# RWKV-style attention and FFN on one core: one reciprocal-root chain per step, and head outputs transposed by DMA

## The reference

```python
xx = jnp.pad(x, ((0, 0), (1, 0), (0, 0)))[:, :T] - x          # token shift
r, k, v = (x + xx*maa_r) @ Wr.T, (x + xx*maa_k) @ Wk.T, (x + xx*maa_v) @ Wv.T
g = silu((x + xx*maa_g) @ Wg.T)
att = rc @ kc * w_mat                                          # per chunk of 64 tokens
yc = att @ vc + rc @ state * wb
new_state = ws * state + kc * wk @ vc
yn = ((y - mu) / sqrt(var + EPS)) * gamma + beta               # per head of 16
x = x + (yn * g) @ Wo.T
x = x + gelu(layernorm(x).astype(f16) @ W0.T + b0).astype(f16) @ W1.T + b1
```

## Time and profile before

| | |
|---|---|
| time, median of 3 runs | 2166.96 µs (2165.43 to 2167.08) |
| the profiled execution's own time | 2165.32 µs |
| its span | 2163.5 µs |
| PE busy | 2073.6 µs (96%) |
| DVE busy | 1874.7 µs (87%) |
| ACT busy | 1169.2 µs (54%) |
| POOL busy | 378.8 µs (18%) |
| DMA queue of SP | 67.9% of the 16 engines' time |
| chain that ended last | PE 52%, DVE 31%, issue 5%, SP's queue 2%, ACT 2% |

### The profile page before, as it was taken

How to read it: one execution, slowest core, us unless ns; L and a number is a source line. 1 busy time by engine, 2 the same in 40 slices (tenths; PEclk the granted TensorE clock), 3 DMA queues, 4 the chain that set the end, 5 groups by cost and what they waited for, 6 DMA issues and landing times.

```text
span 2163.5 us, 58680 instructions
## 1 busy us (share of the span) xinstructions
PE 2073.6 (96%) x24056; PEld 1485.2 (69%) x24056; DVE 1874.7 (87%) x4336; ACT 1169.2 (54%) x1940; POOL 378.8 (18%) x331
## 2 busy tenths in 40 slices
PE   5678999999999999999999999999999999999998
PEld 4456677777667777667777766777776677777665
DVE  6888998888899888889988888998888998888861
ACT  6555455565545565545556554555555455565442
POOL 1111112111111211211121111112111112111120
PEclk8889999999999999999999999999999999999999
DMA  6545667776666777666677766667776667777667
GB/s 206 185 145 158 207 200 224 223 228 201 201 204 206 226 229 220 192 201 208 216 228 223 227 183 210 198 218 229 223 224 186 210 201 222 226 225 206 200 214 238
DMA packets 342987, 452.72 MB, mean 209 GB/s; under 512 B 183872, under 2 KB 221248, under 8 KB 342720
## 3 DMA queue, kind: packets, MB, share of 16 engines
q1 hardware_dynamic: 341088, 448.76, 67.9%
q10 hardware_dynamic: 1632, 0.21, 0.1%
HBM read 316.24 MB, written 25.17 MB: 158 GB/s over the span
## 4 chain that ended last, share of the span: by engine, by line
PE 52%; DVE 31%; issue 5%; SPq 2%; ACT 2%; DMA 1%; DVEq 0%; ACTq 0%
PE F L917 13%; PE F L888 12%; PE sc L719 6%; PE YT L747 6%; DVE mixf L227 6%; DVE att L1114 5%; PE B L719 4%; DVE S L1137 4%; PE YT L719 3%; DVE att L1108 3%; DVE mix L287 3%; DVE kv L1123 2%; PE B L868 2%; DVE gT L1144 1%; DVE dx L218 1%
## 5 line engine op out<-in xcount | busy, mean ns | idle before, releaser
L888 PE MATMUL F<-xT,ring 128*128 128x256 f16 x4096 | 484.9, 273 | 9.2 <-ACT hT L1396 3.6
L917 PE MATMUL F<-ring,hT 128*128 128x512 f16 x2016 | 475.3, 379 | 1.4 <-ACT hT L1396 1.4
L888 PEld LDWEIGHTS F<-xT,ring 128*128 128x128 f16 x4096 | 396.2, 98 | 72.5 <-issue 7.4
L917 PEld LDWEIGHTS F<-ring,hT 128*128 128x128 f16 x2016 | 189.6, 98 | 200.6 <-ACT hT L1396 3.3
L283 ACT ACTIVATE mix<-mixf 128x1024 f16<-128x1024 f32 x128 | 135.2, 1056 | 326.9 <-DVE mixf L227 213.8
L1396 ACT ACTIVATE hT<-F,b,f_rho 128x256 f16<-128x256 f32 x512 | 260.5, 565 | 36.4 <-PE F L888 36.2
L227 DVE SCALAR_TENSOR_TENSOR mixf<-dx,maa,xnT 128x256 f32<-128x256 f32 x512 | 270.7, 556 | 0.4 <-PEq L492 0.3
L719 PE MATMUL B<-mix,WT 128*128 128x256 f16 x2304 | 269.6, 274 | 0.0
L1519 POOL TENSOR_TENSOR Shl<-S,Shl 128x512 f16<-128x512 f32 x128 | 153.8, 1202 | 657.2 <-ACT Shl L1363 657.2
L719 PEld LDWEIGHTS B<-mix,WT 128*128 128x128 f16 x2304 | 223.9, 98 | 36.1 <-issue 0.2
L1363 ACT ACTIVATE Shl<-S 128x512 f16<-128x512 f32 x128 | 80.2, 627 | 239.0 <-DVE S L1137 131.9
(11 more groups left out here) (175 smaller groups left out, 3037.5 us busy)
## 6 DMA issues: line engine op xcount, KB each, us to landing
ring<-w_dram SPq DMA_DIRECT2D x512, 512.0 KB, 4.6
kx<-kT SPq DMA_DIRECT2D x96, 256.0 KB, 2.5
rx<-rT SPq DMA_DIRECT2D x96, 256.0 KB, 4.4
xa<-in_L_attn_x SPq DMA_DIRECT2D x32, 512.0 KB, 7.4
vbd<-vN SPq DMA_DIRECT2D x256, 64.0 KB, 2.8
x<-in_L_attn_x SPq DMA_DIRECT2D x32, 512.0 KB, 5.4
out<-x SPq DMA_DIRECT2D x31, 512.0 KB, 3.9
ring<-in_L_ffn_W SPq DMA_DIRECT2D x10, 512.0 KB, 8.5
```

What stands on the lines that cost most here:

```text
L888: mm = eng.matmul(F[:, j % 2, i * BT:(i + 1) * BT], ring[:, use % RING, i, a * C + kk * P:a * C + (kk + 1) * P], xT[:, :, kk, :], start=(k ...
L917: mm = eng.matmul(F[:, t, :], hT[:, k, rows(t)], ring[:, use % RING, i, a * C:(a + 1) * C], start=(k == 0 and a == 0), stop=(k == NH - 1 a ...
```

## The change

Two things are changed together.

First, the three chains become one. `rs_a`, `rs_r` and `rs_t` hold, side by side, 2 columns for the rows of block n+1, 64 for the heads of block n-1, and 2 for the FFN rows of block n-2. One chain of 11 instructions over 68 columns runs in step n (`dve_power_half`), and one `dve_row_mean` gives both layer norms their offset. So the FFN's mean and root for block n-2, which before were ready at the end of step n-1, come in step n.

Second, in steps 3 to 31 the 8 PE transposes of y go. ACT splits y into half words in `ygT` (`act_y_words`), SP issues a DMA transpose back into `y` (`sp_y_words`), ACT joins the halves in `ygT` (`act_y_join`), and `act_gated` reads `ygT` instead of `sc`. The gate `gT` gets three halves in place of two, since a gate now lives longer. For these steps the orders of ACT, SP and DVE are written anew (`act_steady`, `sp_steady`, `dve_chunks`); PE's order only loses the transposes. In 28 of the 29 steps (3 to 30) there is a block n+1, and so an x to split, transpose and join.

```diff
+    def dve_power_half(eng, n, k):
+        first, last = has(n)
+        if k == 0:
+            eng.wait_ge(s_va, n + 2)
+            if first <= HEADS <= last:
+                eng.wait_ge(s_gn, n)
+        at = slice(EDGES[first], EDGES[last + 1])
+        rsqrt_step(eng, k, s_rs, RSQRT_STEPS * (n + 1), rs_a[:, at], rs_r[:, at], rs_t[:, at])
...
+    def act_y_words(eng, n):
+        eng.wait_ge(s_yn, NT * (n + 1))
+        eng.wait_ge(s_ygl, NT * n)
+        for h in range(2):
+            eng.activation(y_words[:, h * NT * C:(h + 1) * NT * C].rearrange("p (t c) -> p t c", t=NT),
+                           halves(y[:, :, :])[:, :, :, h], ACT.Copy).then_inc(s_yw, 1)
+    def act_y_join(eng, n):
+        eng.wait_ge(s_ywT, 16 * (n + 2 - BY_DMA))
...
+    def act_steady(eng, n, ahead):
+        act_K_hi(eng, n, 0)
+        act_mix_hi(eng, n, 2)
+        act_K_hi(eng, n, 1)
+        act_fnorm(eng, n - 2)
+        act_R_hi(eng, n, 0)
+        if ahead:
+            act_norm(eng, n + 1)
+            act_x_words(eng, n + 1)
+        act_R_hi(eng, n, 1)
+        act_mix_hi(eng, n, 3)
+        act_y_words(eng, n - 1)
+        act_V_hi(eng, n, 0)
+        act_vw_hi(eng, n, 0)
+        act_gelu(eng, n, 0)
+        if ahead:
+            act_x_join(eng, n + 1)
+        act_V_hi(eng, n, 1)
+        act_vw_hi(eng, n, 1)
+        act_gelu(eng, n, 1)
+        act_gelu(eng, n, 2)
+        act_gelu(eng, n, 3)
+        act_y_join(eng, n - 1)
+        act_weights_hi(eng, n, 0)
+        act_gate(eng, n, 0)
+        act_state_hi(eng, n, 0)
+        act_gated(eng, n - 1)
...
+    def sp_y_words(eng, n):
+        eng.wait_ge(s_yw, 2 * (n + 2 - BY_DMA))
+        eng.dma_start_transpose(y_wordsT.rearrange("p (k t) -> p k t", t=P), y_words).then_inc(s_ywT, 16)
+    def sp_steady(eng, n, ahead):
+        use = UNITS * (n - 2) - 4 + RING - 1
+        for i in range(3):
+            sp_weights(eng, use + i)
+        sp_fx(eng, n - 2)
+        sp_kx(eng, n)
+        sp_k_tokens(eng, n)
+        sp_weights(eng, use + 3)
+        if ahead:
+            sp_x_words(eng, n + 1)
+        sp_rx(eng, n)
+        sp_y_words(eng, p)
+        sp_weights(eng, use + 4)
+        sp_weights(eng, use + 5)
+        sp_vbd(eng, n, 0)
...
+    def dve_chunks(eng, n, ahead):
+        if ahead:
+            dve_dx(eng, n + 1)
+            for g in range(G):
+                dve_mix(eng, n + 1, 0, g)
+        dve_weigh(eng, n, 0)
...
+        dve_weigh(eng, n, 1)
+        dve_gated(eng, n - 1)
...
+        dve_take_y(eng, n, 1)
+        dve_residual(eng, n - 1, 1)
+        dve_f_stats(eng, n - 1)
...
-        if tail:
+        if tail and not y_by_dma(n - 1):
             pe_yT(eng, n)
```

More of the change, by code:

```diff
@@ L626, in program @@
     f_bn = sb("f_bn", [P, NT, 6])
-    f_mv = sb("f_mv", [P, NT, 2])
-    fl_a, fl_r, fl_t, fl_n = (sb(f"fl_{c}", [P, NT]) for c in "artn")
     xh = sb("xh", [P, NT, C], F16)
@@ L766, in pe_scores @@
             eng.wait_ge(s_rx, STACK_PER * (n + 1))
-            if due(n):
+            if due(n) and not y_by_dma(n - 1):
                 eng.wait_ge(s_af, G * n)
@@ L1142, in dve_gate @@
         eng.wait_ge(s_tg, 2 * n + half + 1)
[L1143 to L1144 removed]
+        at = gate_at(n, half)
+        eng.scalar_tensor_tensor(out=gT[:, at, :, :], in0=gT[:, at, :, :], scalar=1.0,
                                  in1=B[:, :].rearrange("p (g t) -> p g t", g=2),
@@ L1197, in dve_step, with mixing @@
     def dve_step(eng, n):
         att_n, tail, ff, ahead, late = in_step(n)
+        early = n <= 2
+        mixes = [(m, g) for m in (2, 3) for g in range(G)] if att_n else []
+        def mixing(count):
+            for _ in range(min(count, len(mixes))):
+                dve_mix(eng, n, *mixes.pop(0))
+        if n <= nb + 1:
+            if early:
+                mixing(G)
+            if ahead:
+                dve_stats(eng, n + 1, 0)
+            mixing(1)
+            if tail:
+                dve_variance(eng, n - 1, 1)
+            if ahead:
+                dve_stats(eng, n + 1, 1)
+            if att_n and early:
+                dve_K_lo(eng, n, 0)
+            if ahead:
+                for t in range(NT):
+                    dve_mean_var(eng, n + 1, t)
+            mixing(1)
+            if tail:
+                dve_head_var(eng, n - 1)
+            dve_row_var(eng, n)
+            if att_n and early:
+                mix_lo(eng, n, 2)
+            mixing(1)
+            for k in range(RSQRT_STEPS):
+                dve_power_half(eng, n, k)
+                if att_n:
+                    if k == 1 and not early:
+                        dve_K_lo(eng, n, 0)
+                    elif k == 6:
+                        dve_K_lo(eng, n, 1)
+                    elif k == 8 and not early:
+                        mix_lo(eng, n, 2)
+                    else:
+                        mixing(1)
+            dve_row_mean(eng, n)
+            if tail:
+                for t in range(NT):
+                    dve_normalized(eng, n - 1, t)
@@ L1224, in dve_step @@
         if att_n:
-            if not early:
-                mix_lo(eng, n, 2)
             dve_R_lo(eng, n, 0)
@@ L1249, in dve_step @@
             dve_e(eng, n - 3)
-        if tail:
+        if tail and not y_by_dma(n - 1):
             dve_gated(eng, n - 1)
+        if tail and y_by_dma(n - 1):
+            dve_chunks(eng, n, ahead)
+            return
         if n < 2:
@@ L1542, in pool_step @@
                 pool_state_lo(eng, n, c)
+                if c == 0 and tail and y_by_dma(n - 1):
+                    pool_gated_lo(eng, n - 1)
     def sp_weights(eng, use):
@@ L1620, in sp_step @@
             sp_weights(eng, use + 4)
-        if ahead and n >= 2:
+        if ahead and n == BY_DMA - 1:
             sp_x_words(eng, n + 1)
```

261 lines of the change are left out of this document (154 added, 107 removed).

## The result

The changed kernel takes 2283.4 µs (median of 4, 2278.8 to 2290.1), the kernel before 2167.0 (median of 4, 2165.4 to 2168.7): a ratio of 1.054, 95% interval 1.051 to 1.057. It is slower by 116 µs. The forecast was 2301, its range 2200 to 2365.

What follows compares the result with a forecast made beforehand. PE was taken to set the pace, busy 63.09 of 63.37 µs a step. A net 3.4 plus 1.5 of clock over 28 steps gave 137; 2165.3 + 137 - 1 = 2301 µs, range 2200 to 2365.

Steps and rivals of the forecast that it cites:

- The shared mean: On DVE: the single chain's mean is there between 1081.3 and 1082.3, taken as 1082.2; 9.4 µs later for the FFN.
- The issue of x: In SP's queue, behind xh: the transpose of x is issued at 1090.6, only 1.3 µs earlier than before.
- The landing: DMA transpose of x: lands the median 7.3 µs after issue, at 1097.9, between 1096.7 and 1099.6.
- Rival C: x lands 4.63 µs after its start, `rx` no longer in flight; net 0.7 µs a step, 2184; chance 0.07.
- What stands behind it on ACT: After x lands: join 2.44, V tile 1 and its weighted copy 1.01, gelu 1 1.01; 4.5 µs in all.
- The wait of PE: Ahead of up 3: PE stands 4.7 µs for gelu 1, and up 3 starts at 1102.4, not 1098.6.
- The clock: PE's granted clock falls behind the wait, losing 1.5 µs in each step, bounds 0 and 2.4.
- Rival A: The waits come as forecast but the clock stays at 2.4 GHz: 94 µs more, 2259; chance 0.25.
- PE's gain: In each step PE loses y's transposes, 0.87 µs, and the wait for DVE's low weights, 0.42 µs.
- The sum: Per step: 3.4 µs net lengthening plus 1.5 of clock, 4.9 µs; 137 µs over 28 steps.
- the tail: First three steps and tail get other orders: between 5 µs less and 5 more, taken as 0.
- `rx` and the unit of up 4: SP's later items: both hidden, `rx` by the new wait alone (1.4 µs without it), the unit by 1.5 µs.

Runs made afterwards that it cites:

- experiment 4: Shared chain alone, y transposed on PE in every step and the old mid-step orders kept, against the kernel before: 2205.6 µs, 1.017.
- Experiment 2: Changed kernel plus 14 filler matmuls on PE between up 2 and up 3: 2250.0 µs, 1.038 against the kernel before.
- experiment 1: Changed kernel with ACT's join of x moved behind gelu 1: 2221.8 µs, 1.024 against the kernel before.
- experiment 7: Kernel of 3 with the ring unit of up 4 issued ahead of the transposes for `kN` and y: 2210.0 µs, 1.019 against the kernel before.
- 3: Changed kernel with x's transpose issued right behind `kx` and that for `kN` only behind `rx`: 2173.5 µs, 1.003 against the kernel before.
- experiment 8: Kernel of experiment 7 with the join of x behind gelu 1 and the tail's ring units ahead of xh's transpose: 2218.7 µs, 1.024 against the kernel before.

## Why the prediction was right

The direction, the place and the mechanism held, and the time lies in the range; the forecast is 18 µs (0.8%) high. That it is so close is in part luck. For the 28 steps it had 29 µs too many (137 against 108). Of these, 7 were made up outside these steps, where it expected 1 less and 6 more were measured, and 5 by the median, which lies that much above the profiled execution. By its own steps:

- **The shared mean** was to be there 12.35 µs into the step (1082.2 in a step that begins at 1069.85). Measured 12.33 (1068.00 + 0.16 in one that begins at 1055.83). Right.
- **The issue of x**: predicted 20.75 into the step, measured 20.9. Right.
- **The landing**: here the size was off. I took the 7.3 of the earlier trace rows and measured 5.7. The row of before was of a transpose with the copies to `rx` and the unit of up 4 between it and the unit of up 3; with both gone both its issue (3.66 instead of 4.63) and its landing are shorter, and experiment 4, which keeps the old order, has 7.6 again (300 to 2000 µs). Which of the two it was no run separates. The experiments show for `kN` and y too that the landing goes by what was issued ahead. Rival C had this mechanism, for `rx` alone, and took it too far (4.63).
- **What stands behind it on ACT**: predicted 4.5 µs from landing to up 3, measured 4.6 (1082.54 to 1087.09). Right.
- **The wait of PE**: predicted 4.7, measured 3.66 on average, 1.0 less. In the step shown it is 1.4 less, as x lands that much earlier into the step.
- **The clock**: predicted 1.5 a step for every step. Experiment 2 gives 1.2; the 28 groups of up 3 show 0.84 on average in that group alone, all of it in 21 of them. Rival A (no loss of clock) is out.
- **PE's gain** of 0.87 and 0.42 was counted right in its sign: the transposes are gone, and so is DVE's wait, which was 0.2 a step on average and not 0.42 (5.0 µs in 27 steps).
- **The sum**: 4.9 a step predicted, 3.9 measured. As wait, gain and clock it is 3.66 - 0.87 - 0.2 + 1.2 = 3.8.
- **Not seen**: the tail, which I took at 0 with 5 µs either way. Its wait for the ring grew from 0.95 to 4.74, since the units stand behind xh there, and the part from step 31 on is 4.1 longer.
- **Counted as nothing, and right**: ACT's four new passes. `rx` and the unit of up 4 were to be hidden by the new wait. They were, and by little else: once experiment 1 takes it away, PE waits for both. For `rx` I had given 1.4 µs a step without the wait, and 3.9 in all were measured, in 8 steps; for the ring I had given nothing without it, and 18.2 were measured. The prediction also didn't ask what of x's late landing reaches DVE once PE no longer waits for gelu 1: the gate's 20.1.

What stays open is what makes a landing longer. In experiment 7, against 3, `kN` was issued 1.2 µs later and took 1.1 longer to land, and PE waited 1.2 for it in each step; no run separates the share of the unit ahead from that of other traffic. Nor was each of the two parts tried with a queue order of its own that was best for it.

## What to carry to other kernels

When work is taken from the engine that sets the pace and given to DMA, write down for the one issuing queue when each item is issued and lands, and what on each engine stands behind the instruction that waits for it. A join belongs behind everything whose result is needed before the landing, and no later: in experiment 8 it went behind gelu 1 although x had long landed, and DVE was late instead. Fusing small chains over several consumers makes the earliest consumer wait for the latest producer: here 2.2 µs of DVE a step, which was no bound, were saved (1603.6 to 1543.1 in 28 steps, experiment 4), and the transpose of xh began 4.6 µs later in the step (13.9 against 9.3), what stands behind it in SP's queue about 1.5. In these runs a transpose landed soonest right behind another or behind the copies to `kx`, and latest right behind large loads, so time a landing in the order in which it will be issued.
